# Two streams of batches in one order: the loop over rounds unrolled, the lag 150 units and not 60, and the FP4 rounding by addition

## The reference, cut to what matters

```python
x = _layernorm(x + _L0_attn_ref(x, ...))      # 16 heads of 8, causal, and a second, linear attention
x = _layernorm(x + _L0_xattn_ref(ctx_1024, x, ...))   # 8 heads of 64
x = _layernorm(x + _L0_ffn_ref(x, ...))       # 16 experts that attend
x = _layernorm(x + _L1_attn_ref(x, ...))      # 16 heads of 8, causal
x = _layernorm(x + _L1_xattn_ref(x, ctx_1024, ctx_1024, mask, ...))
x = _layernorm(x + _L1_ffn_ref(x, ...))       # one shared and eight routed experts
x = _layernorm(x + _L2_attn_ref(x, ...))      # sampled positions
x = _layernorm(x + _L2_xattn_ref(x, ctx_1024, ctx_1024, ...))
x = _layernorm(x + _L2_ffn_ref(x, ...))       # 8 heads choose 8 of 1024 experts by product keys
x = _layernorm(x + _L3_attn_ref(x, ...))      # 16 heads of 8, rotary
x = _layernorm(x + _L3_xattn_ref(x, ctx_1024, ...))   # 8 heads of 64
x = _layernorm(x + _L3_ffn_ref(x, ...))       # FP4 values in all three products
```

```python
_GRID = [0.0, 0.5, 1.0, 1.5, 2.0, 3.0, 4.0, 6.0]
_MID = [0.25, 0.75, 1.25, 1.75, 2.5, 3.5, 5.0]
scale = maximum(max(abs(xb)) / 6.0, 1e-12)
xn = xb / scale
idx = searchsorted(_MID, abs(xn))
q = _GRID[idx] * sign(xn) * scale
...
h = silu(fp4_linear(x, w_gate)) * fp4_linear(x, w_up)
return fp4_linear(h, w_down)
```

## Time and profile before

| | us |
|---|---|
| median of three runs | 3567.33 |
| the profiled execution's own time | 3561.01 |
| its span | 3559.4 |
| TensorE (PE) busy | 2892.6 (81%) |
| VectorE (DVE) busy | 1941.3 (55%) |
| ScalarE (ACT) busy | 1026.6 (29%) |
| GpSimd (POOL) busy | 518.5 (15%) |
| mean granted clock of TensorE, of full speed | 0.822 |

### The profile page before, as it was taken

One profiled execution on the slowest core, in us unless ns is written; L12 is line 12 of the kernel. 1 busy time (PEld: TensorE's weight loads), 2 busy tenths in 40 slices (PEclk: granted clock), 3 DMA queues, 4 the chain that ended last, 5 costly groups with the idle time before them and its releaser, 6 DMA issues.

```text
span 3559.4 us, 40665 instructions
## 1 busy us (share of the span) xinstructions
PE 2892.6 (81%) x14625; PEld 1569.7 (44%) x14625; DVE 1941.3 (55%) x5029; ACT 1026.6 (29%) x2060; POOL 518.5 (15%) x801
## 2 busy tenths in 40 slices
PE   5899998879987667898468999988799786678884
PEld 2235566324543543255323356563345445433562
DVE  6443425644655987525654433356446559875355
ACT  2431212353332101551134221113533320025410
POOL 1220000121112441000012100011201125300000
PEclk9998978889887677896679988878899776788955
DMA  4000000000000000000010000000000000000000
GB/s 151 2 1 1 1 1 23 24 1 19 30 12 1 0 24 25 1 1 1 3 65 2 1 1 1 1 23 24 1 19 30 12 1 0 24 25 1 1 1 6
DMA packets 16431, 49.74 MB, mean 14 GB/s; under 512 B 1761, under 2 KB 8801, under 8 KB 14434
## 3 DMA queue, kind: packets, MB, share of 16 engines
q1 hardware_dynamic: 15650, 45.79, 3.8%
q10 hardware_dynamic: 576, 1.29, 0.1%
HBM read 45.43 MB, written 1.05 MB: 13 GB/s over the span
## 4 chain that ended last, share of the span: by engine, by line
PE 32%; DVE 10%; ACT 4%; issue 3%; SPq 1%; POOL 0%; DMA 0%; ACTq 0%; POOLq 0%; DVEq 0%
PE psum L964 4%; PE psum L549 2%; PE psum L952 2%; PE psum L519 2%; DVE keep_s L2201 1%; PE psum L539 1%; PE psum L936 1%; PE psum L932 1%; PE psum L711 1%; PE psum L1482 1%; ACT PT_s L615 1%; PE psum L1312 1%; DVE fs_v_s L2063 1%; PE psum L1774 1%; DVE mx_s L678 1%
## 5 line engine op out<-in xcount | busy, mean ns | idle before, releaser
L615 ACT ACTIVATE PT_s<-psum 128x512 f32<-128x512 f32 (+3 forms) x768 | 340.5, 495 | 246.4 <-PE psum L539 243.2
L675 DVE CUSTOM_DVE_ANT_0 rest_s<-psum,packed_early 128x128 f32<-128x128 f32 (+3 forms) x512 | 225.2, 487 | 159.5 <-PE psum L525 158.0
L381 POOL TENSOR_SCALAR ve<-mv 128x4 f32<-128x4 f32 x48 | 14.4, 299 | 1958.0 <-DVE mv L371 1957.8
L2106 PE MATMUL psum<-packed_early,keep_s 128*128 128x128 f32 x1024 | 183.9, 341 | 124.2 <-DVE keep_s L2201 124.0
L987 ACT ACTIVATE PT_s<-psum 128x512 f32<-128x512 f32 (+1 forms) x224 | 121.2, 592 | 424.8 <-PE psum L954 424.8
L539 PE MATMUL psum<-QS_s,KS_s 64*128 64x512 bf16 (+3 forms) x768 | 197.1, 350 | 48.7 <-DMA QS_s<-nmT_s 34.5
L525 PE MATMUL psum<-KS_s,QS_s 64*128 64x512 bf16 (+3 forms) x768 | 187.0, 355 | 47.6 <-DVE mx_s L678 27.2
L2106 PEld LDWEIGHTS psum<-packed_early,keep_s 128*128 128x128 f32 x1024 | 152.3, 177 | 162.3 <-DVE keep_s L2201 148.1
L2063 POOL TENSOR_TENSOR buffer<-sim_s 128x1024 f32<-128x1024 f32 x80 | 187.3, 2354 | 240.4 <-DVE keep_s L2201 238.2
L964 PEld LDWEIGHTS psum<-vaug0x_s,PT_s 128*128 128x128 f32 (+1 forms) x1280 | 187.7, 231 | 61.1 <-ACT PT_s L987 47.2
L964 PE MATMUL psum<-vaug0x_s,PT_s 128*128 128x65 f32 (+1 forms) x1280 | 194.1, 315 | 24.2 <-ACT PT_s L987 20.4
(11 more groups left out here) (443 smaller groups left out, 5461.4 us busy)
## 6 DMA issues: line engine op xcount, KB each, us to landing
buffer<-packed_experts SPq DMA_DIRECT2D x36, 384.0 KB, 3.4
buffer<-packed_moe SPq DMA_DIRECT2D x4, 2048.0 KB, 10.0
buffer<-packed_cross SPq DMA_DIRECT2D x4, 2048.0 KB, 8.2
buffer<-packed_product SPq DMA_DIRECT2D x4, 1024.0 KB, 4.8
packed_early<-packed_early SPq DMA_DIRECT2D x1, 2654.5 KB
raw_s<-packed_setup SPq DMA_DIRECT2D x1, 1840.0 KB, 7.9
packed_late<-packed_late ACTq DMA_DIRECT2D x4, 314.0 KB, 3.8
QS_s<-nmT_s SPq DMA_DIRECT2D x72, 8.0 KB
```

The source lines that it names most:

```text
L615: a.activation(PT[:, u // 4 % 2, i, q0_of(c):T], bank[u % 3][:, q0_of(c):T], ACT.Exp, scale=scale).then_inc(exp_done.sem, 1)
L675: v.tensor_tensor_reduce(junk[:, u % 2, 0:w], bank[n % 4][:, 0:w], s.w["causal"][:, T - w:T], 1.0, -3e38, ALU.add, ALU.max, mx[:, j, h:h + ...
L2106: mm = pe.matmul(CT[:, c * P:(c + 1) * P], keep[:, n % KEPT, c * P:(c + 1) * P], s.w["ident"][:], is_transpose=True, start=(h == 0 and c % ...
```

## The change

The hardware loop goes. Each stream's two batches are written out behind each other, so the order on each engine is one piece from the first batch to the last; the barrier and the clearing of semaphores stand once, at the end. Stream 1 starts at unit 150 of the common order and not at 60. `load_batch` becomes two programs: `fetch_batch` issues the transfers of the next batch (x, context, mask, expert weights) at the start of the previous batch's l3_ffn, as soon as that stream's norm before it is done, into the other of two tiles for x; `turn_batch` stands where the batch begins, waits on VectorE for the previous batch's last norm, and turns x. The tile for the raw mask becomes a part of `att`, which makes room for the second x. The expert semaphores count on over the turns.

`quantise` no longer compares. The block maximum comes from one reduction by absolute value, the inverse scale is multiplied by a number just below one (ties go down), and the scaled values are rounded to the grid by adding and subtracting a number that depends on their exponent: an integer "and" takes the exponent bits, one instruction makes from them 1.5 x 2^22 times the power of two, not below 1.5 x 2^22. That is 10 links for 16; the sign needs none. l3_ffn's unit times are set closer: it is 33 units long and not 54, so a batch is 1087 units. The whole order is 2 x 1087.4 + 150 = 2325 units long; two rounds were 2 x 1168 = 2337.

```diff
@@ -21,8 +22,8 @@
 LATE_LOADS = 4
 STREAMS = 2
 SIGNALS = 40
-LOADS = 6
-LAG = 60.0
+LOADS = 12
+LAG = 150.0
 
 Q_SLOTS = (0, 0, 1, 0, 2, 1)
 K_SLOTS = (0, 1, 0, 2, 0, 1)
...
+def fetch_batch(s, t, x, batch, free):
+
+    x_loaded, mask_loaded, moe_loaded = s.load_signals(3)
+    s.fetched, s.moe_loaded = (x_loaded(32), mask_loaded(16)), moe_loaded(16)
+
+    def sync(sp):
+        yield 0
+        if free is not None:
+            sp.wait_ge(*free)
+        sp.dma_start(x[:], t["x"][batch].rearrange("(j p) d -> p j d", p=P)).then_inc(x_loaded.sem, 16)
+        sp.dma_start(s.ctx[0:LC, :], t["ctx_1024"][batch]).then_inc(x_loaded.sem, 16)
+        sp.dma_start(s.mask_rows[0:TJ, :], t["mask_Bx1xSx1_fk0"][batch].rearrange("o (j p) e -> (o j) (p e)", p=P)).then_inc(mask_loaded.sem, 16)
+        sp.dma_start(s.buffer[:, 0:t["moe"].shape[1]], t["moe"]).then_inc(moe_loaded.sem, 16)
+
+    return Program(0.0, sync=sync)
+
+
+def turn_batch(s, t, x, batch, free):
 
     s.new_stage()
     cleared, turned, xT_ready, mask_ready = s.signals(cleared=1, turned=2, xT_ready=1, mask_ready=1)
-    x_loaded, mask_loaded, rest_loaded, moe_loaded = s.load_signals(4)
-    s.x_ready, s.xT_ready, s.rest_loaded, s.moe_loaded = x_loaded(32), xT_ready(1), rest_loaded(32), moe_loaded(16)
-    raw_mask = s.mask_rows
+    rest_loaded, = s.load_signals(1)
+    x_loaded, mask_loaded = s.fetched
...
+        y = t["x"][batch]
+        sp.dma_start(s.x_next[:, 0:TJ - 1, :], y[1:T - P + 1, :].rearrange("(j p) d -> p j d", p=P)).then_inc(rest_loaded.sem, 16)
+        sp.dma_start(s.x_next[0:P - 1, TJ - 1, :], y[T - P + 1:T, :]).then_inc(rest_loaded.sem, 16)
 
     def vector(v):
         yield 0
+        if free is not None:
+            v.wait_ge(*free)
         v.memset(s.x_next[96:P, TJ - 1, :], 0.0).then_inc(cleared.sem, 1)
...
-def quantise(link, v, src, mag, units, mask, block_max, inv, out):
+def quantise(link, v, src, scaled, power, block_max, inv, out):
 
     rows, n = src.shape
     blocks = lambda t_: t_.rearrange("p (b q) -> p b q", q=16)
     spread = lambda t_: t_.unsqueeze(2).to_broadcast([rows, n // 16, 16])
-    link(v.scalar_tensor_tensor(mag, src, -1.0, src, ALU.mult, ALU.max))
-    link(v.tensor_reduce(block_max, blocks(mag), AX_X, ALU.max))
+    link(v.tensor_reduce(block_max, blocks(src), AX_X, ALU.max, apply_absolute_value=True))
     yield
     link(v.tensor_scalar(block_max, block_max, 1.0 / 6.0, 1e-12, ALU.mult, ALU.max))
     link(v.reciprocal(inv, block_max))
-    link(v.tensor_tensor(blocks(mag), blocks(mag), spread(inv), ALU.mult))
+    link(v.tensor_scalar(inv, inv, TIES_DOWN, None, ALU.mult))
+    link(v.tensor_tensor(blocks(scaled), blocks(src), spread(inv), ALU.mult))
     yield
-    link(v.tensor_scalar(units, mag, 5.0, 2.0, ALU.is_gt, ALU.mult))
-    for mid in (3.5, 2.5):
-        link(v.scalar_tensor_tensor(units, mag, mid, units, ALU.is_gt, ALU.add))
+    link(v.tensor_scalar(power.bitcast(I32), scaled.bitcast(I32), EXPONENT_BITS, None, ALU.bitwise_and))
+    link(v.tensor_scalar(power, power, ROUNDER, ROUNDER, ALU.mult, ALU.max))
     yield
-    link(v.tensor_scalar(mask, mag, 1.75, None, ALU.is_gt))
-    link(v.scalar_tensor_tensor(units, units, 2.0, mask, ALU.mult, ALU.add))
+    link(v.tensor_tensor(scaled, scaled, power, ALU.add))
+    link(v.tensor_tensor(scaled, scaled, power, ALU.subtract))
     yield
-    for mid in (1.25, 0.75, 0.25):
-        link(v.scalar_tensor_tensor(units, mag, mid, units, ALU.is_gt, ALU.add))
-    yield
-    link(v.tensor_scalar(mask, src, 0.0, 1.0, ALU.is_ge, ALU.mult))
-    link(v.scalar_tensor_tensor(units, mask, -0.5, units, ALU.add, ALU.mult))
-    yield
-    link(v.tensor_tensor(blocks(out), blocks(units), spread(block_max), ALU.mult))
-
-
-QUANTISE_LINKS = 16
+    link(v.tensor_tensor(blocks(out), blocks(scaled), spread(block_max), ALU.mult))
+
+
+QUANTISE_LINKS = 10
+TIES_DOWN = 1.0 - 2.0 ** -24
+EXPONENT_BITS = 0x7F800000
+ROUNDER = 1.5 * 2.0 ** 22
...
-    TX = (0.0, 8.0)
-    TURN = (8.0, 17.0)
-    GATED = (16.0, 18.0, 20.0, 22.0)
-    UP = (11.0, 16.7, 18.7, 20.7)
-    TH = (26.0, 38.0)
-    end = 54.0
+    TX = (0.0, 3.5)
+    TURN = (4.5, 9.0)
+    GATED = (7.0, 9.5, 11.5, 13.5)
+    UP = (5.5, 8.5, 10.5, 12.5)
+    TH = (15.0, 22.0)
+    end = 33.0
...
-            s.x = sb("x", [P, TJ, D])
+            s.x_tiles = [sb("x", [P, TJ, D]) for _ in range(2)]
...
-            s.mask_rows = sb("mask_rows", [P, P])
+            s.mask_rows = s.att[:, 0, :]
...
-        xout = t["out"].rearrange("(q s) (j p) d -> s q p j d", s=STREAMS, p=P)
-        with nc.Fori(0, B // STREAMS) as pair, nc.allow_non_contiguous_dma("rows of a batch"):
-            for s in streams:
-                s.late_loaded = (late_loaded, 16 * LATE_LOADS)
-                s.levels, s.next_load = [0] * SIGNALS, 0
-                s.expert_loaded = [Signal(sem, 0) for sem in s.expert_sems]
-                s.programs = [load_batch(s, t, pair)]
+        for s in streams:
+            s.late_loaded = (late_loaded, 16 * LATE_LOADS)
+            s.next_load = 0
+            s.programs = []
+            free = None
+            for turn in range(B // STREAMS):
+                batch = turn * STREAMS + s.index
+                slots = [sum(1 for e in range(EXPERTS) if e % EXPERT_SLOTS == i) for i in range(EXPERT_SLOTS)]
+                s.expert_loaded = [Signal(sem, 16 * turn * n) for sem, n in zip(s.expert_sems, slots)]
+                if turn == 0:
+                    s.programs.append(fetch_batch(s, t, s.x_tiles[turn % 2], batch, None))
+                s.programs.append(turn_batch(s, t, s.x_tiles[turn % 2], batch, free))
                 for i, stage in enumerate(STAGES):
+                    last = i == len(STAGES) - 1
                     if stage is l1_attn:
                         s.programs.append(load_experts(s))
                     elif stage is l2_attn:
                         s.programs.append(load_product(s, t["product"]))
                     elif stage is l3_attn:
                         s.programs.append(load_cross3(s, t["cross3"]))
+                    elif last and turn + 1 < B // STREAMS:
+                        s.programs.append(fetch_batch(s, t, s.x_tiles[(turn + 1) % 2], batch + STREAMS, s.x_ready))
                     programs, branch, ready = stage(s)
                     s.programs += programs
-                    last = i == len(STAGES) - 1
-                    s.programs.append(add_norm(s, branch, ready, out=xout[s.index, bass.ds(pair, 1)].rearrange("o p j d -> p (o j) d") if last else None))
+                    s.programs.append(add_norm(s, branch, ready, out=t["out"][batch].rearrange("(j p) d -> p j d", p=P) if last else None))
+                free = s.x_ready
+        with nc.allow_non_contiguous_dma("rows of a batch"):
...
-            numbers = [sem.num for s in streams for sem in s.all_sems]
-            assert sorted(numbers) == list(range(min(numbers), max(numbers) + 1))
-            nc.all_engine_barrier(sems_to_clear=range(min(numbers), max(numbers) + 1))
+        numbers = [sem.num for s in streams for sem in s.all_sems]
+        assert sorted(numbers) == list(range(min(numbers), max(numbers) + 1))
+        nc.all_engine_barrier(sems_to_clear=range(min(numbers), max(numbers) + 1))
```

81 lines of the change are left out of this document (36 added, 45 removed).

## The result

The changed kernel takes 3596.10 us, median of 14 runs (3586.33 to 3621.67), the kernel before on the same chip 3571.43 (3565.81 to 3575.34): a ratio of 1.0086 [1.0065, 1.0106]. It is slower by 25 us, where 3450 was predicted; the range (3370 to 3530) does not hold it. The profiled execution took 3601.0 us, its span is 3598.9.

A forecast was written before the change was run, and what follows sets the result against it. TensorE was taken to bound the joint stretches, latency of short VectorE instructions the single-stream ones. Setup 27, head 100, joint 3196 and tail 175 made 3498, less 52 is 3446, called 3450 us (chance 0.60); range 3370 to 3530.

The forecast's parts named there:

- the new neighbours: In the joint part, the two streams' l2_ffn no longer meet at lag 150: 52 us less, bounds 0 and 104.
- Setup, quantise, l3_ffn alone: Setup ends at 27 us, one quantisation of 704 columns takes 6.7 us for 12.5, lone l3_ffn 42 us for 58.
- The boundary: Between the rounds, barrier, loop branch and first transfers go; the 71 + 37 us of single streams there become joint time.
- The lag: Head and tail become 150 units long and not 60: head 100 us, tail 175 us (bounds 148 and 220).
- the upper bound, 145: The head's 150 units at the pace of the joint stretch take 145 us; the lower bound, at single pace, was 93.
- The bound of 126: In the tail, l3_xattn's attention takes at most the whole window of 126 us; 60 at full clock, 85 was taken.
- TensorE's busy time: Whole kernel: total stays at 2892.6 us because the clock holds; a move of over 60 us would prove the forecast wrong.
- The rule on the port: In l2_ffn, VectorE and GpSimd collisions between streams vanish: up to 52 us over two rounds, left to the better-mixture rival.
- The rule on the clock: By this rule alone the tail's attention would run at 2.4 GHz, the sum 25 us lower; the profile row was kept instead.
- The ends eat the gain: Rival, chance 0.11 at 3530 us: head 145, tail 220, no gain from neighbours, 3588 at worst; or next batch held, 3520.
- The order's misfit: Rival, chance 0.07 at 3630 us: l2_ffn's transposes, waiting for VectorE's selection, hold up ready TensorE work, 132 us added.
- The better mixture: Rival, chance 0.22 at 3390 us: all joint time at TensorE share 0.867, and VectorE slowed less by GpSimd.

The follow-up runs named there:

- c150old: The changed kernel with the old rounding and the old unit times of l3_ffn, chains and lag 150 kept: 3629.89 us, ratio 1.0190 to the kernel before.
- c60: The changed kernel with the lag set back from 150 to 60 units, all else kept: 3501.61 us, ratio 0.9804 to the kernel before.
- w150h: The changed kernel with 90 added matmuls of 512 columns, result unused, in stream 1's track in units 60 to 150: 3595.24 us, ratio 1.0066 to before.
- w150t: The changed kernel with 150 added matmuls of 512 columns, result unused, behind stream 0's last program: 3599.02 us, ratio 1.0087 to before.

## Why the prediction was wrong, point by point

The sum was made of 27 for setup, 100 for the head, 3196 - 52 for the joint part and 175 for the tail, 3446. The span is 27 + 137 + 3212 + 223 = 3599. So of the 153 us between them the head has 37, the tail 48, the new neighbours 52, and the rest of the joint part 16.

*Setup, quantise, l3_ffn alone: right.* Setup ends at 27; ten instructions take 6.6 us where 6.7 was worked out; l3_ffn alone lasts from the norm's last scaling at 3549.0 to 3590.5, 41.5 us for 42. At a lag of 60 the rounding brings 35 us, where 6 in setup and 32 in l3_ffn's two lone stretches make 38. Whether the three l3_ffn beside other work gain nothing, as was counted, isn't settled: c150old has 34 for the 22 that stand alone, to some 15 us.

*The boundary: right in kind.* No window without the other stream lies in the middle, and the chains bring 34 us at the old lag.

*The lag: the step that failed.* In the prediction's words, the head and tail "that remain are 150 units long and not 60". Their place and number were right and both were priced too low, 137 for 100 and 223 for 175. In the head I put the 90 added units at (100 - 37) / 90 = 0.70 us each; they cost 99 / 90 = 1.10. They are the second half of an attention with heads of 8 wide and the start of l0_attn. From 70 to 135 us TensorE is busy 45.1 of 65 at clock 0.50. From the start of its batch to l0_attn stream 0 needs 27.0 to 132.7, 105.7 us, all alone; before, with stream 1 beside it from 70 us on, it needed 33.0 to 140.8, 107.8 us. Alone it is hardly faster than beside the other stream; the upper bound, 145, stood on that pace. I took a value near the lower one because l0_attn is dense, and so left the attention at the pace of the first 60 units. In the tail two terms fell short: the rest of the l3 attention, the same kind of work, 58.8 us for 27, and l3_xattn, 110 with its norm for 85 and 6. The bound of 126 for its attention held, and 85 was too near the other. l3_ffn with its norm, 46.1 for 48, and the end, 8.4 for 9, were right.
A comparison was missing: what a unit of lag costs alone, twice, against what it costs jointly, once. Measured it is 99 / 90 = 1.10 at the head, (222.9 - 107.4) / 90 = 1.28 at the tail and 1.57 jointly, so 0.81 us for each unit, 73 of the 94.5 us; the rest is the slower pace of the joint part, 25 us between the two spans. The prediction's own terms give 0.70 + (175 - 55) / 90 (55: the tail of 71 us with l3_ffn 16 shorter) - 1654 / 1048 = 0.70 + 1.33 - 1.58 = 0.45, a loss of 41 us. The sum never showed it: it went from the whole kernel's busy time to a total, in which the lag's loss and the boundary's gain could not be seen apart.

*The new neighbours: failed.* It was a gain of 52 us and, against a lag of 60, there was none. Its sign that was asked for came: the stretch with VectorE at 0.89 and TensorE at 0.66 is gone, and TensorE waits 72.2 us for the selection and not 124.0. But in the two stretches of a round where a stream is in l2_ffn TensorE is idle 44.4 and 38.4 us, in both rounds 166 (the second round's stretches, 159 us with 116.3 busy and 150 with 109.5, repeat the first's); with lag 60, where the stages overlap, it is idle 85.8 and 86.6, 172. Two stretches with VectorE at 0.84 and 0.79 have taken the place of one at 0.85. Over the joint part TensorE's idle time is 535 us at 150 and 548 at 60, with 4% fewer units: what the selection no longer holds up is given back one by one, for instance L979 for ScalarE 22.5 to 37.0 us, L2323 for VectorE 19.0 to 37.0, L540 for VectorE 29.7 to 40.2. (These are over the whole kernel; in the joint part alone they are 22.5 to 35.8, 9.6 to 27.6 and 29.7 to 40.2.) Against the paces at 30 and 90 units, 1.609 and 1.597, the changed kernel's 1.586 would be a gain of 47 and 22 us; as the pace moves up and down with the lag, no part of it can be put down to the parted l2_ffn. The waits of c60 that these are read against:

```profile
PE psum L2121 <- DVE keep_s L2216: 131.3, 64, 5.3
...
PE psum L540 <- DVE mx_s L693: 29.7, 30, 2.9
...
PE psum L979 <- ACT PT_s L1002: 22.5, 23, 1.2
...
PE psum L2323 <- DVE h_s L2263: 19.0, 6, 8.2
```

*TensorE's busy time: not constant.* I held it and said that a move of over 60 us would be wrong. It moved by 60.5 against before. Against lag 60 the ends hold 265.9 us of it for what there takes 96.3 in the ends and 104.4 more in the joint part: 65 us more for the same work, at clocks of 0.73 and 0.62 in the ends instead of 0.83.

*The rule on the port.* By the Trainium skill (SBUF — State Buffer, section "Who interferes with whom") a VectorE instruction with two SBUF inputs waits for a GpSimd instruction that reads SBUF, or the other way round. The prediction worked out up to 52 us from it, from its own rows, for the parted l2_ffn. On VectorE part of that came: l2_ffn's sums and selections (L2078, L2216) take 253.2 us in the changed kernel and 277.4 in c60, 24 us less. Of the 48 sums 14 take over 1.4 us in either kernel, and these are shorter in the changed one; the median is 1218 ns in both. That agrees with the rule; that the port is the reason isn't shown. The sum's rows, c60 first:

```profile
L2078 DVE TENSOR_TENSOR fs_v_s<-sim_s 128x1024 f32<-128x1024 f32 x48 | 80.0, 1667 | 0.2
L2078 DVE TENSOR_TENSOR fs_v_s<-sim_s 128x1024 f32<-128x1024 f32 x48 | 70.6, 1471 | 0.0
```

TensorE's idle time in the stretches of l2_ffn, 172 and 166 us, shows little of it, and the total nothing.

*The rule on the clock.* The Trainium skill (TensorE: Matmul & The Clock Gate, section "What's actually happening") lets the clock follow TensorE's activity. In w150h added matmuls lift it from 0.50 to 0.92, which agrees. The share of busy time alone doesn't tell it: the tail's 3434 to 3545 is 84% busy at 0.65.

*The rivals.* "The ends eat the gain" was what happened. It had the right place, ends of 145 and 220 where 137 and 223 came, and 3588 at its worst; with a chance of 0.11 it was forecast near its half-way point, at 3530. Its other part, a next batch held until stream 1 ends, did not come. It also took TensorE's busy time as constant, and from it the joint part: 3196 us for the 3212 measured. The order's misfit did not come about: waits for the selection fell. The better mixture did not either.

## What to carry to other kernels

A lag between two streams is paid at both ends and refunded once in the middle, so price it by the unit (alone at the head, plus alone at the tail, less joint) before looking at which stages it brings together. Then run the lags around the chosen one: here the pace of the joint part moved by up to 2% from lag to lag, as much as the price of the lag, and no figure forecast from other lags held. If an end is worked out by bounds, find which stage fills the added units and take its own row, not the mean of the units before it. When a change has three parts that can be set apart by one line each, expect that one of them may hide the others: here two gains of 34 us each stood behind a loss of 94.5.

## What the runs showed of the hardware that was not expected

TensorE can be busy most of the time and stay near the lower of its two levels, 1.2 GHz, as the prediction's row of 36.7 busy in 40 us at 0.67 already had it: from 3434 to 3545 us it is busy 92.8 of 111 us at a mean clock of 0.65, and from 70 to 135 us 45.1 of 65 at 0.50. More than half of the first is matmuls over 64 or 77 rows, its largest groups (times, busy us, mean ns | idle us):

```profile
L979 PE MATMUL psum<-vaug3x_s,PT_s 77*128 77x65 f32 x128 | 24.2, 366 | 6.5 <-ACT qT3x_s L1005 5.4 <-ACT PT_s L1002 1.2
L967 PE MATMUL psum<-qT3x_s,kT3x_s 64*77 64x512 f32 x32 | 14.2, 978 | 0.7 <-ACT nmT_s L995 0.7
L951 PE MATMUL psum<-kT3x_s,qT3x_s 64*128 64x77 f32 x128 | 13.8, 381 | 0.9 <-DVE vaug3x_s L1207 0.9
```

Whether the rows or something else of them matter wasn't tried on their own. Sixty added matmuls of 512 columns and 128 rows in the latter stretch brought 0.92, but 47 of them in the former, in w150t, only 0.69. And one binary's time moved by 2.2% with the clock it was granted (3509.6 us at 0.826, 3586.6 at 0.804, ten runs), though another, with ten units more of lag, stayed within 0.45% (3493.5 to 3508.8, five runs).
